# Moving statistics, row transposes, high parts and the first output to other places in the queues of an attention kernel (512-query chunks)

## The reference

```python
xn = layernorm(x)                                  # over the last axis, eps 1e-5
q, k, v = xn @ wq.T + bq, xn @ wk.T + bk, xn @ wv.T + bv
attn = softmax(q @ k.T * 256 ** -0.5)
ffn = xn @ W.T + b + xn @ (up_aux @ (lora_up @ (lora_down @ down_aux))).T
return x + attn @ v + ffn
```

## Time and profile before

| what | value |
|---|---|
| timed runs | 573.47 to 575.7 us, median 574.85 |
| profiled execution | 573.26 us, its span 571.5 us |
| TensorE busy | 526.7 us, 92% of the span |
| VectorE, ScalarE, GpSimd busy | 367.4, 276.0, 373.6 us |
| mean granted TensorE clock | 0.979 of 2.4 GHz |

### The profile page before, as it was taken

One profiled execution on the slowest core, in us unless ns is written; L12 is line 12 of the kernel. 1 busy time (PEld: TensorE's weight loads), 2 busy tenths in 40 slices (PEclk: granted clock), 3 DMA queues, 4 the chain that ended last, 5 costly groups with the idle time before them and its releaser, 6 DMA issues.

```text
span 571.5 us, 8131 instructions
## 1 busy us (share of the span) xinstructions
PE 526.7 (92%) x2948; PEld 454.5 (80%) x2948; DVE 367.4 (64%) x838; ACT 276.0 (48%) x589; POOL 373.6 (65%) x222
## 2 busy tenths in 40 slices
PE   5997879899799998999899997999979999999987
PEld 4786768888678887788788886788867888888877
DVE  4769946759367672767648585485845847475682
ACT  3745385350944527454472535725267262734340
POOL 3812877755888755878559777596695966661650
PEclk9999899999999997999989999999989999999998
DMA  8110022000040001400022000500003000000001
GB/s 243 36 46 0 2 74 112 1 37 1 7 178 1 38 0 39 146 2 37 1 97 88 23 16 1 179 6 38 0 1 111 2 38 1 37 2 6 32 1 73
DMA packets 8694, 25.04 MB, mean 44 GB/s; under 512 B 1850, under 2 KB 3792, under 8 KB 7760
## 3 DMA queue, kind: packets, MB, share of 16 engines
q1 hardware_dynamic: 7328, 24.38, 11.8%
q10 hardware_dynamic: 1328, 0.16, 0.2%
HBM read 16.15 MB, written 8.39 MB: 43 GB/s over the span
## 4 chain that ended last, share of the span: by engine, by line
PE 51%; DVE 25%; ACT 12%; issue 5%; POOL 3%; ACTq 0%; POOLq 0%; DVEq 0%
PE g_ps L942 8%; PE g_ps L944 7%; PE g_ps L943 7%; DVE s L815 6%; PE s_ps L942 6%; PE s_ps L944 6%; PE s_ps L943 6%; PE o_ps L1033 4%; ACT stat_cols L606 4%; ACT s L633 4%; PE o_ps L1035 3%; PE o_ps L1034 3%; ACT prod L590 3%; DVE tile_max L782 3%; DVE tile_max_t L787 2%
## 5 line engine op out<-in xcount | busy, mean ns | idle before, releaser
L492 POOL TENSOR_TENSOR p_lo<-s,p_hi 128x1024 fp32r<-128x1024 f32 x60 | 142.5, 2405 | 46.4 <-ACT p_hi L640 46.4
L1033 PE MATMUL o_ps<-v_hi,p_hi 128*128 128x258 f32 x480 | 138.8, 289 | 6.7 <-DVE base L831 4.8
L1035 PE MATMUL o_ps<-v_hi,p_lo 128*128 128x258 f32 x480 | 136.3, 284 | 0.0
L1034 PE MATMUL o_ps<-v_lo,p_hi 128*128 128x256 f32 x480 | 136.0, 283 | 0.0
L633 ACT ACTIVATE s<-s,e 128x512 f32<-128x512 f32 x128 | 84.3, 714 | 94.7 <-DVE s L815 94.5
L1033 PEld LDWEIGHTS o_ps<-v_hi,p_hi 128*128 128x128 f32 x480 | 91.6, 191 | 13.9 <-DVE base L831 10.3
L1034 PEld LDWEIGHTS o_ps<-v_lo,p_hi 128*128 128x128 f32 x480 | 92.3, 192 | 1.3
L1035 PEld LDWEIGHTS o_ps<-v_hi,p_lo 128*128 128x128 f32 x480 | 91.6, 191 | 0.0
L942 PE MATMUL s_ps<-xt_hi,zt_hi 128*128 128x512 f32 x192 | 75.4, 392 | 2.2 <-DVE zt_lo L745 1.6
L943 PE MATMUL s_ps<-xt_lo,zt_hi 128*128 128x512 f32 x192 | 74.8, 390 | 0.0
L944 PE MATMUL s_ps<-xt_hi,zt_lo 128*128 128x512 f32 x192 | 74.8, 390 | 0.0
(11 more groups left out here) (142 smaller groups left out, 1055.2 us busy)
## 6 DMA issues: line engine op xcount, KB each, us to landing
out<-base SPq DMA_DIRECT2D x15, 512.0 KB, 2.6
x_sb<-in_L_attn_x SPq DMA_DIRECT2D x7, 1024.0 KB, 8.4
x_t<-in_x_t SPq DMA_DIRECT2D x6, 1024.0 KB, 6.4
x_sb<-in_L_attn_x SPq DMA_DIRECT2D x4, 256.0 KB, 6.6
out<-base SPq DMA_DIRECT2D x4, 128.0 KB, 1.9
s<-in_L_attn_wk SPq DMA_DIRECT2D x1, 256.0 KB, 3.2
s<-in_L_attn_wq SPq DMA_DIRECT2D x1, 256.0 KB, 6.2
s<-in_L_attn_wv SPq DMA_DIRECT2D x1, 256.0 KB, 6.9
```

What stands on the lines that cost most here:

```text
L492: nc.gpsimd.tensor_tensor(p_pair(g, p_lo_sb, j), s_pair(j), p_pair(g, p_hi_sb, j).bitcast(f32), ALU.subtract).then_inc(p_lo_made, 1)
L1033: nc.tensor.matmul(o[:, 0:D + ONES], hi, v_hi[i][:, n, :], start=first, stop=False)
L1034: nc.tensor.matmul(o[:, 0:D], hi, v_lo[i][:, n, :], start=False, stop=False)
L1035: mm = nc.tensor.matmul(o[:, 0:D + ONES], lo, v_hi[i][:, n, :], start=False, stop=last)
```

## The change

It reorders instructions in the queues; none is added or taken away.

- Groups of batch 1: `FIRST` now puts transposes 0 and 1 after score tile 1, 2 and 3 after P x V 1, z groups after P x V 2 and 3; v groups as in `LATER`.
- Statistics of batch b+3 are made in the odd turn (c = 1) of batch b; those of batch 2 in turn 0.
- rstd of b+3 stands between the two `make_xt_lo(b+2, .)`.
- Columns of b+2 follow `p_hi` in the even turn (as before in the code, but for rstd a turn old); those of batch 2 follow `make_e(1)`.
- Rows (`make_stat_rows`) follow `make_groups_lo(b, c, 0)`.
- `make_out(b, c*QT)` follows the second shift.
- In chunk 0 `p_hi` follow each pair of exponentials; the block maximum is split from `make_top`, and a low part stands between.

```diff
+        V_GROUPS = {0: (8, 9), 1: (10, 11), 2: (12, 13), 3: (14, 15)}
-        FIRST = [{1: (0, 1), 2: (2, 3), 3: (4, 5)}, {0: (6, 7), 1: (8, 9, 10), 2: (11, 12, 13), 3: (14, 15)}]
-        LATER = [{1: (4, 5), 2: (6, 7)}, {0: (8, 9), 1: (10, 11), 2: (12, 13), 3: (14, 15)}]
+        FIRST = [{0: (0, 1), 1: (2, 3), 2: (4, 5), 3: (6, 7)}, V_GROUPS]
+        LATER = [{1: (4, 5), 2: (6, 7)}, V_GROUPS]
...
# GpSimd, loop over b
                 make_p_lo(CHUNKS * b)
-                if b + 2 < B:
-                    make_rstd(b + 2, 0)
                 shift_raw(CHUNKS * b + 1)
+                if b == 0:
+                    make_rstd(EARLY, 0)
...
                     norm_x_t(b + 2, 1)
-                    for h in range(2):
-                        make_xt_lo(b + 2, h)
+                    make_xt_lo(b + 2, 0)
+                    if b + 3 < B:
+                        make_rstd(b + 3, 0)
+                    make_xt_lo(b + 2, 1)
...
# ScalarE
             make_p(0, 1)
+            make_p_hi(0, 0)
             make_p(0, 2)
             make_group_hi(0, 2 * NT + 7)
-            for i in range(3, TILES):
-                make_p(0, i)
+            make_p(0, 3)
+            make_p_hi(0, 1)
+            for j in range(2, PAIRS):
+                make_p(0, 2 * j)
+                make_p(0, 2 * j + 1)
+                make_p_hi(0, j)
             for g in range(LAST):
...
-                make_p_hi(g, 0)
+                if g > 0:
+                    make_p_hi(g, 0)
                 make_raw(g + 1, 0)
-                make_p_hi(g, 1)
+                if g > 0:
+                    make_p_hi(g, 1)
                 make_groups_hi(b, c, 0)
                 make_raw(g + 1, 1)
-                make_p_hi(g, 2)
-                make_p_hi(g, 3)
-                if c == 0 and b + 2 < B:
+                if g > 0:
+                    make_p_hi(g, 2)
+                    make_p_hi(g, 3)
+                if c == 0 and 0 < b < B - 2:
                     make_stat_cols(b + 2)
...
                     make_e(b + 1)
+                    if b == 0:
+                        make_stat_cols(EARLY)
...
# VectorE
             make_tile_max(0, 7)
+            make_block_max(0)
+            make_group_lo(0, 2 * NT + 4)
             make_top(0)
-            make_group_lo(0, 2 * NT + 4)
...
                 make_tile_max(g + 1, 0)
+                make_tile_max(g + 1, 1)
+                make_groups_lo(b, c, 0)
                 if b + 2 < B and c == 1:
                     make_stat_rows(b + 2)
-                make_tile_max(g + 1, 1)
-                make_groups_lo(b, c, 0)
-                if b + 2 < B and c == 0:
-                    dve.wait_ge(x_loaded[b % 2], DMA * ((b + 3) // 2))
-                    make_stats(b + 2, range(2))
+                if g == 0:
+                    dve.wait_ge(x_loaded[0], DMA)
                 for n in range(2, TILES):
                     make_tile_max(g + 1, n)
-                    if b + 2 < B and c == 0 and n < TILES - 1:
-                        make_stats(b + 2, range(n, n + 1 if n < TILES - 2 else TILES))
-                        make_mean_var(b + 2, range(n - 2, n - 1 if n < TILES - 2 else TILES - 2))
+                    if g == 0:
+                        make_stats(EARLY, range(n - 2, n - 1 if n < TILES - 1 else TILES))
+                make_block_max(g + 1)
                 make_top(g + 1)
-                if g + 1 == LAST:
-                    make_out(b, c * QT)
                 shift(g + 1, 0)
                 shift(g + 1, 1)
-                if b + 2 < B and c == 0:
-                    make_mean_var(b + 2, range(TILES - 2, TILES))
+                make_out(b, c * QT)
                 for i in range(2, HELD):
                     shift(g + 1, i)
-                if g + 1 < LAST:
-                    make_out(b, c * QT)
                 make_out(b, c * QT + 1)
                 make_groups_lo(b, c, 1)
+                if c == 0 and b == 0:
+                    make_mean_var(EARLY)
+                if c == 1 and b + 3 < B:
+                    dve.wait_ge(x_loaded[(b + 3) % 2], DMA * ((b + 4) // 2))
+                    make_stats(b + 3, range(TILES // 2))
                 make_out(b, c * QT + 2)
+                if c == 1 and b + 3 < B:
+                    make_stats(b + 3, range(TILES // 2, TILES))
+                    make_mean_var(b + 3)
```

More of the change, by code:

```diff
@@ L783, in make_tile_max, with make_block_max @@
                                                    tile_max[:, :], ALU.add, ALU.max).then_inc(tile_max_made, 1)
-            def make_top(g):
+            def make_block_max(g):
                 dve.wait_ge(tile_max_made, TILES * (g + 1))
@@ L790, in make_top @@
                                         AXIS, ALU.max).then_inc(block_max_made, 1)
+            def make_top(g):
                 dve.wait_ge(block_max_made, g + 1)
```

## The result

The changed kernel takes 542.97 us (median of 542.16 to 543.78) against 575.18 for the kernel before, beside which it ran; the ratio is 0.9445, 95% interval 0.9417 to 0.9473. The profiled execution took 543.78 us, its span is 542.0 us. That is the slowest of its four executions.

What follows compares the result with a forecast made beforehand. TensorE bounds the kernel, so only its idle and low-clock time can be won: 571.5 + 2.8 - 31.5 - 0.7 - 0.55 = 541.6 us of span, 543.3 as profiled execution, median 544.9 us. Range 538 to 553.5.

Steps and rivals of the forecast that it cites:

- Batches 1 to 5, -31.5: Main loop: z, odd-turn and output stalls and the low clock go; five batches take 311.65 us against 343.11.
- Batch 6, -0.7: Last batch with both turns free of statistics: its output stalls go, 63.01 us becoming 62.33.
- The start, +2.8: Turns 0 and 1: new TensorE stalls of 3.0 and 4.2 us, with 3.4 us lost to the clock; 2.8 us longer.
- The end, -0.55: Turn 14: output behind two shifts lets the last exponentials and high parts begin sooner, 0.55 us less.
- First output: Output 0 behind the second shift: its stalls of 0.24 to 0.50 us, plus 0.1 for refilling, go in both turns.
- The early `p_hi`, credited with 1.8 us of waits for `p_lo`: Turn 0: `p_hi` after each pair of exponentials ends 1.8 us of waits for `p_lo`.
- Block maximum: 0: Turn 0: splitting it gives v group 12 its low part 2 us sooner, but the next scores still wait: 0.
- B (clock): Rival: TensorE's clock stays low as long as now, 8.5 us of half clock come back: 553 us; chance 0.08.
- C: Rival: VectorE does not catch up after the rows, 1.9 us per odd turn before v group 10: 556; chance 0.07.
- D: Rival: the start costs 4 to 8 us more as high parts or columns chain into turn 2: 549 to 552; chance 0.05.

Runs made afterwards that it cites:

- run 3: Changed kernel with statistics, mean and variance and rstd of batches 3 to 7 back in the even turn: 571.15 us.
- run 7: Changed kernel with the column copies behind the first two exponentials in even turns of batches 1 to 5, rstd still early: 547.43 us.
- run 8: Kernel before plus only the early statistics, rstd and columns, all other parts at their old places: 552.40 us.
- run 4: Changed kernel with batch 2's statistics, rstd and columns moved into idle time of turn 0: 537.08 us.
- run 2: Changed kernel with only the first output back behind all six shifts: 555.77 us.
- run 9: Changed kernel with only chunk 0's `p_hi` back behind all eight exponentials: 542.54 us.
- run 5: Changed kernel with only the groups of batch 1 back in their old places: 540.75 us.
- run 10: Changed kernel with only the low part of v group 12 back behind the whole of top in chunk 0: 543.56 us.
- run 1: Changed kernel with only the row transposes back in front of the second maximum and v's low parts: 545.88 us.
- run 6: As run 4, statistics among maxima 2 to 5 of turn 0, and the transposes' high parts behind the second `p_hi` of chunk 0: 532.62 us.

## Why the prediction was right, point by point

- *Batches 1 to 5, -31.5.* Measured -31.3 (311.83 against a forecast 311.65). The mechanism was right, and runs 3, 7 and 8 show its parts: the late rstd, the stall, and the clock behind it. That it came out to 0.2 us in 312 has luck in it. Without the output's stalls batch 6 fell to 62.00 us, not to 62.33, while the batches with rows take 62.37: a gain of 0.33 per batch that I had not counted and a cost of 0.37 for the rows, which I had put at nothing, cancel.
- *Batch 6, -0.7.* 62.00 instead of 63.01: -1.0. A removed output stall of 0.24 us gave 0.5, not the 0.34 that I took; the term of 0.1 us for refilling was too small.
- *The start, +2.8.* Measured +4.8. The stalls were right (3.17 and 4.26 against 3.0 and 4.2; the two small ones 0.35 and 0.47 against 0.9 and 0.8). Mis-sized was the clock: 3.4 + 6.8 us at half, of which the first 1.9 lie inside the stall itself (low from 98.49, TensorE back at 100.39), so 4.2 lost, not 3.4. Besides, this execution's turn 0 began at 51.16, 0.7 later than before. The remaining 0.5 us and what the small stalls fell short of I did not take apart. That the columns in front of `p_hi(1,0)` make the second stall is shown by run 4.
- *The end, -0.55.* Measured -1.9 (40.0 instead of 42.0 us after batch 6). 1.7 of it is the halved stretch at 557.3 of before, which this execution has not; I had not counted it. The stall of 0.82 fell to 0.40, the next stayed at 0.89, so of the 0.55 I get 0.2 to 0.4.
- *First output.* Its cover was mis-sized: I priced it by the regular turns' 0.24 to 0.50 us. Run 2 shows that in the new arrangement the place is worth 12.8 us: some 7 in the regular turns, at 0.6 instead of 0.34, and some 4 at the ends, where stalls of 2.26 and 3.07 us stand without it.
- *The early `p_hi`, credited with 1.8 us of waits for `p_lo`.* This step failed: undone (run 9) those waits do not come back. With batch 1's groups in their old places the term holds: run 5 has no wait for `p_lo`, and run 8, which has the late `p_hi` beside them, has two, of 1.9 us together. In their new places the stall of 2.6 to 3.2 us stands in front and gives GpSimd its time, so I had counted a gain that another part of the change takes away. It is worth nothing here.
- *Block maximum: 0.* Run 10 agrees.
- *Rivals.* B (clock) did not happen in batches 1 to 6, but the clock fell at the start. Batches 1 to 6 still have stalls of 0.1 to 0.4 us at a clock of 1.00. The rule of the Trainium skill on short idle spells (TensorE: Matmul & The Clock Gate, A second HAM failure mode) does not show at that rate. C is there at 0.3 us per odd turn, not 1.9, and at the place that it named. D is the direction in which the start missed.

The sum (541.6 us of span, 542.0 measured) is nearer than its terms: +2.0 at the start and -1.4 at the end cancel, by luck. The median is 1.9 us below the forecast of 544.9, because I took it to be 1.6 above the profiled execution; here it is 0.8 below it.

The undoing of three parts (runs 1 to 3) costs 2.9 + 12.8 + 28.2 = 43.9 us together, more than the 32.2 gained. Some 2 of it are no true undoing, as run 2 makes the last turn worse than it was before the change; the rest says that the parts cover for each other. The price of taking one away is not what it adds alone.

Open: why a stall of about the same length is followed by 3.4, 6.8 or no microseconds at half clock. The executions of one kernel differ by it too: those of the changed kernel are 543.78 and 543.70 us at a mean clock of 0.991, and 542.23 and 542.16 at 0.994.

## What to carry to other kernels

Look in the trace for a turn that lacks the suspected work: its length is a good forecast, for it has the clock and what follows each stall in it. It does not hold what the work still costs in its new place, here 0.3 us per odd turn. Before moving a block of instructions, check that its new place is idle in the first and the last turn too. Nearly all that this change lost, it lost in the first two turns: high parts behind a full queue of ScalarE (3.2 us, run 6), and 4 us of copies with `p_hi` queued behind them (4.3 us, run 4). And price a removed stall with the clock behind it: here 14.1 us of stalls were worth 23.

## What of the hardware I had not expected

The halved clock can begin before a stall is over: in run 3 it is low from 288.6, and the stall ends at 289.68, so part of such a stretch costs nothing. Its even turns with 6.8 us at half take 34.2 to 34.4 us, those with 3.4 take 33.4: some 1.0 more, not 1.7. And a stall of 3.2 us at the same place of turn 0 was followed by 6.8 us at half (run 4), by 3.4 (the changed kernel) and by none (run 7, where it ends at 60.93):

```profile
60.90:64.40 3.50, 3.47 (x15) 2.89 (x16) 3.35 (x7) 0.00 (x0) 0.17 (x1) 1.00 0.02 5
```
